# Token groups laid out by batch row and quarter of the steps, one transfer per load, reload and store, in a mixture-of-experts and gated recurrence kernel

## The reference

```
def _L0(x, t_emb, ...):              # on all 8192 tokens
    shared = silu(xf @ w1) * (xf @ w3) @ w2
    s = sigmoid(concat([xf, tf]) @ router_W)
    _, topk_idx = top_k(s + router_bias, 2)      # 2 of 8 experts per token
    gates = s_sel / s_sel.sum()
    h = gelu(einsum('nc,ech->enh', xf, W1e)); y = einsum('enh,ehc->enc', h, W2e)
    return (shared + einsum('ne,enc->nc', combine, y)) / 3
def step(h, z_t):                    # 256 steps in order, all batch rows at once
    gate = sigmoid(h @ Wh.T + z_t @ Wz.T + b)
    h_new = tanh(h * leak + gate * z_t)
    return h_new, h_new
x = x + _L0(x, cond);  x = x + hs    # hs: the states of all steps, z = x
```

## Time and profile before

| | |
|---|---|
| time of three runs | 1169.03, 1170.54, 1175.3 us; median 1170.54 |
| the profiled execution | 1181.83 us, its span 1179.8 us |
| busy in the profiled execution | PE 804.2, DVE 564.8, ACT 452.5, POOL 261.4 us |
| mean granted TensorE clock | 0.837 |
| transfers | 129.65 MB, of them 64 + 64 + 128 issues of x_tok, x_res and out_dram |

### The profile page before, as it was taken

One profiled execution on the slowest core, in us unless ns is written; L12 is line 12 of the kernel. 1 busy time (PEld: TensorE's weight loads), 2 busy tenths in 40 slices (PEclk: granted clock), 3 DMA queues, 4 the chain that ended last, 5 costly groups with the idle time before them and its releaser, 6 DMA issues.

```text
span 1179.8 us, 25116 instructions
## 1 busy us (share of the span) xinstructions
PE 804.2 (68%) x8750; PEld 561.1 (48%) x8750; DVE 564.8 (48%) x2038; ACT 452.5 (38%) x1321; POOL 261.4 (22%) x286
## 2 busy tenths in 40 slices
PE   0655944465974694698379478845958999859653
PEld 0322743443573562367267245734724688425332
DVE  3652413324762352667136357633536754547543
ACT  2341522222542351445145144523524566424333
POOL 1236005615006115100700510052052000340000
PEclk9877976778987797998679798876989999969765
DMA  9683775527344332453542334443334154330001
GB/s 268 183 263 119 190 169 131 157 85 170 68 96 152 95 104 79 105 122 83 147 95 88 93 83 94 92 125 91 86 107 99 39 116 119 112 85 28 10 10 37
DMA packets 203498, 129.65 MB, mean 110 GB/s; under 512 B 138578, under 2 KB 192372, under 8 KB 203380
## 3 DMA queue, kind: packets, MB, share of 16 engines
q1 hardware_dynamic: 188260, 86.03, 30.7%
q0 software_dynamic: 14400, 41.96, 11.1%
q10 hardware_dynamic: 720, 0.05, 0.0%
HBM read 39.90 MB, written 56.62 MB: 82 GB/s over the span
## 4 chain that ended last, share of the span: by engine, by line
PE 41%; another core or an unknown queue 16%; DVE 13%; issue 11%; SPq 8%; ACT 8%; DMA 3%; DVEq 0%; ACTq 0%
PE bank L1525 40%; SPq L797 5%; SPq L779 2%; DVE taken L1359 2%; DVE pre L1362 2%; DVE hid_low L1312 1%; ACT th L1065 1%; ACT hs_high L1073 1%; DMA x_res<-in_x_dram 1%; DVE r_part L1326 1%; PE bank L1693 1%; DVE full L1296 1%; ACT half L1031 1%; DVE left L1214 1%
## 5 line engine op out<-in xcount | busy, mean ns | idle before, releaser
L1525 PE MATMUL bank<-xe,w1e_high 128*128 128x128 f16 x1408 | 235.9, 227 | 45.9 <-issue 26.9
L1359 DVE SCALAR_TENSOR_TENSOR taken<-th,zq 128x64 f32<-128x64 f32 x256 | 57.4, 224 | 301.0 <-ACT th L1065 289.1
L1525 PE MATMUL bank<-xs,w_high 128*128 128x512 f16 x512 | 182.0, 403 | 21.7 <-DVE full L1296 17.5
L1065 ACT ACTIVATE th<-bank 128x64 f32<-128x64 f32 x256 | 56.9, 222 | 330.1 <-PE bank L1525 171.4
L1525 PE MATMUL bank<-hs_high,gwt_high 128*128 128x32 f16 x1024 | 80.6, 180 | 135.2 <-ACT hs_high L1073 106.3
L1525 PE MATMUL bank<-xe,w1e_low 128*128 128x128 f16 x704 | 157.8, 227 | 14.2 <-issue 14.2
L1312 DVE TENSOR_TENSOR hid_low<-full,hid_high 128x512 f16<-128x512 f32 x152 | 104.7, 689 | 120.8 <-ACT hid_high L1018 109.5
L1525 PEld LDWEIGHTS bank<-xe,w1e_high 128*128 x1408 | 123.5, 101 | 75.5 <-issue 59.5
L1525 PEld LDWEIGHTS bank<-hs_high,gwt_high 128*128 128x128 f16 x1024 | 70.5, 99 | 178.7 <-ACT hs_high L1073 129.5
L924 POOL TENSOR_TENSOR fence_pool<-zero 128x1 f32<-128x1 f32 x12 | 2.7, 227 | 673.9 <-issue 246.9
L1073 ACT ACTIVATE hs_high<-pre 128x64 f16<-128x64 f32 x256 | 65.6, 256 | 124.8 <-DVE pre L1362 113.6
(11 more groups left out here) (151 smaller groups left out, 1746.9 us busy)
## 6 DMA issues: line engine op xcount, KB each, us to landing
y_slots_even<-y_pair SPq DMA_DIRECT2D x44, 256.0 KB
y_slots_odd<-y_pair SPq DMA_DIRECT2D x44, 256.0 KB
x_tok<-in_x_dram SPq DMA_DIRECT2D x64, 128.0 KB, 2.9
x_res<-in_x_dram SPq DMA_DIRECT2D x64, 128.0 KB
out_dram<-o_tok SPq DMA_DIRECT2D x128, 64.0 KB
x_slots_even<-zeros POOLq DMA_DIRECT2D x1, 3072.0 KB, 14.8
x_slots_odd<-zeros POOLq DMA_DIRECT2D x1, 3072.0 KB, 11.7
y_got<-in_L_cond_W1e_dram SPq DMA_DIRECT2D x4, 512.0 KB
```

Source lines behind the costliest of these rows:

```text
L1065: nc.scalar.activation(flat3(th[:, s % 2]), gate_sums(s), ACT.Tanh, scale=0.5 / UP).then_inc(s_th, 1)
L1359: dve.scalar_tensor_tensor(flat3(taken[:, s % 2]), flat3(th[:, s % 2]), 1.0, flat3(z_of(s // HALF)[:, s % HALF]), ALU.add, ALU.mult).then_ ...
L1525: return pe.matmul(out_ap, w, mov, start=start, stop=stop, skip_group_check=True)
```

## The change

A tile's partition is now 4 times the batch row plus the quarter t of the group's 16 steps, and tile j of a group holds steps 4t + j. So partition p of a group is four steps in a row of one batch row, 4 KB in DRAM: the load, the reload and the store (2 KB a partition there) are one transfer each, with all 128 partitions. Semaphore counts follow (16 instead of 64 for each group). Where z leaves PSUM and where o_ch is written, the order of tokens is turned back into steps by the access pattern of the same instruction: the innermost loop over the batch rows steps 4 f32 elements in PSUM (`by_token`), and o_ch is written with that step. On SP, `load_res` moves from behind the pair store to the head of the unit. The four tables are written anew; the numbers of operations are the same.

```diff
-    x_in = x.rearrange("b (j t) c -> t b j c", t=TT)
-    out_v = out.rearrange("b (a j t) c -> a t b j c", j=2, t=TT)
+    x_in = x.rearrange("b (q t j) c -> q b t (j c)", t=TT, j=GROUP)
+    out_v = out.rearrange("b (a t j) c -> a b t (j c)", t=TT, j=2)
-        cond_t = sb("cond_t", [P, KC, TT, NB])
+        cond_t = sb("cond_t", [P, KC, NB, TT])
-        o_ch = sb("o_ch", [P, KC, HALF, NB])
+        o_ch = sb("o_ch", [P, KC, 2, NB, TT])
+        def by_step(ap):
+            return ap.rearrange("p (t j) b -> p t j b", j=GROUP)
+        def by_token(bank):
+            return bank[:].rearrange("p (j b t) -> p t j b", b=NB, t=TT)
             def load_x(q):
-                for t in range(TT):
-                    sp.dma_start(x_tok[NB * t:NB * (t + 1), q % NXT, :, :], x_in[t][:, q * GROUP:(q + 1) * GROUP, :]
-                                 ).then_inc(s_x[q % NXT], 16)
+                sp.dma_start(x_tok[:, q % NXT].rearrange("p j c -> p (j c)"), x_in[q]).then_inc(s_x[q % NXT], 16)
             def load_res(q):
-                for t in range(TT):
-                    sp.dma_start(x_res[NB * t:NB * (t + 1), :, :], x_in[t][:, q * GROUP:(q + 1) * GROUP, :]
-                                 ).then_inc(s_res, 16)
+                sp.dma_start(x_res[:].rearrange("p j c -> p (j c)"), x_in[q]).then_inc(s_res, 16)
             def store(c):
-                for t in range(TT):
-                    sp.dma_start(out_v[c, t], o_tok[NB * t:NB * (t + 1), c % 2, :, :]).then_inc(s_out[c % 4], 16)
+                sp.dma_start(out_v[c], o_tok[:, c % 2].rearrange("p j c -> p (j c)")).then_inc(s_out[c % 4], 16)
             def body(u):
+                for q in range(N_GROUPS):
+                    if u.i == FINISH[q] - 2:
+                        load_res(q)
                 if u.kind == EXPERT and u.k + NIN < PAIRS[u.n]:
                     load_pair(u.n, u.k + NIN)
                 prepare(u.i)
                 done = units_at(u.i - DOWN_LAG, EXPERT)
                 if done:
                     store_pair(done)
-                for q in range(N_GROUPS):
-                    if u.i == FINISH[q] - 2:
-                        load_res(q)
...
-                    nc.scalar.activation(zq[:, q % NZQ, :, kc, :], y_ps[kc][:].rearrange("p (t b) -> p t b", b=NB),
+                    nc.scalar.activation(by_step(zq[:, q % NZQ, :, kc, :]), by_token(y_ps[kc]),
                                          ACT.Copy, scale=HALVED).then_inc(s_part if q < EARLY else s_z, 1)
...
-                part = zq[:, q % NZQ, :, kc, :]
-                dve.scalar_tensor_tensor(part, gate_ps[kc][:].rearrange("p (t b) -> p t b", b=NB), HALVED, part,
+                part = by_step(zq[:, q % NZQ, :, kc, :])
+                dve.scalar_tensor_tensor(part, by_token(gate_ps[kc]), HALVED, part,
                                          ALU.mult, ALU.add).then_inc(s_z, 1)
...
-                    ins = dve.scalar_tensor_tensor(o_ch[:, kc], z_of(c)[:, :, kc, :], 2.0,
-                                                   hist[:, some, kc, :], ALU.mult, ALU.add)
+                    ins = dve.scalar_tensor_tensor(o_ch[:, kc].rearrange("p j b t -> p t j b"),
+                                                   z_of(c)[:, :, kc, :].rearrange("p (t j) b -> p t j b", j=2), 2.0,
+                                                   hist[:, some, kc, :].rearrange("p (t j) b -> p t j b", j=2),
+                                                   ALU.mult, ALU.add)
...
-                                                o_ch[:, kc, j * TT:(j + 1) * TT, :].rearrange("p t b -> p (t b)"),
+                                                o_ch[:, kc, j].rearrange("p b t -> p (b t)"),
```

and of the tables, for example in PE_AT:

```diff
-    (34, 8): ((FILL, 0), (STEP, 0),), (35, 4): ((FILL, 1),), (35, 5): ((STEP, 1),), (36, 0): ((STEP, 2),),
+    (34, 7): ((FILL, 0),), (35, 0): ((STEP, 0), (FILL, 1),), (35, 1): ((STEP, 1),), (35, 4): ((STEP, 2),),
```

More of the change, by code:

```diff
@@ new lines @@
+    (43, 11): ((REST, 17),), (44, 2): ((MIX, 18),), (44, 6): ((REST, 18),), (44, 12): ((MIX, 19),),
+    (45, 7): ((REST, 19),), (45, 10): ((MIX, 20),), (45, 12): ((REST, 20),), (46, 6): ((MIX, 21),),
+    (47, 2): ((REST, 21), (MIX, 22), (REST, 22),), (47, 6): ((MIX, 23),), (47, 7): ((REST, 23),),
+    (49, 2): ((MIX, 24), (Z, 7), (REST, 24), (MIX, 25),), (49, 4): ((REST, 25),), (50, 4): ((MIX, 26),),
+    (50, 8): ((REST, 26),), (50, 9): ((MIX, 27),), (51, 2): ((REST, 27),), (51, 7): ((MIX, 28),),
@@ new lines @@
+    (70, 7): ((MIX, 62),), (70, 9): ((REST, 62),), (70, 11): ((MIX, 63),), (71, 1): ((REST, 63),),
+    (71, 10): ((MIX, 64),), (71, 11): ((Z, 12), (REST, 64),), (72, 2): ((MIX, 65),), (72, 8): ((REST, 65),),
+    (72, 13): ((MIX, 66),), (73, 4): ((REST, 66),), (73, 7): ((MIX, 67),), (73, 8): ((REST, 67),),
+    (73, 10): ((MIX, 68),), (73, 12): ((REST, 68),), (74, 3): ((MIX, 69),), (75, 0): ((REST, 69),),
+    (75, 5): ((MIX, 70), (REST, 70),), (76, 0): ((MIX, 71),), (77, 5): ((REST, 71), (MIX, 72),),
@@ new lines @@
+    (77, 8): ((Z, 13), (REST, 72),), (78, 2): ((MIX, 73), (REST, 73), (MIX, 74), (REST, 74),),
+    (78, 4): ((MIX, 75), (REST, 75),), (79, 2): ((MIX, 76),), (79, 4): ((REST, 76),),
+    (79, 7): ((MIX, 77), (REST, 77),), (80, 1): ((MIX, 78), (REST, 78), (MIX, 79),), (80, 9): ((REST, 79),),
+    (81, 1): ((MIX, 80), (REST, 80), (MIX, 81), (REST, 81),), (81, 4): ((MIX, 82),), (81, 6): ((REST, 82),),
+    (82, 1): ((MIX, 83),), (82, 3): ((REST, 83), (MIX, 84), (REST, 84), (MIX, 85), (REST, 85),),
@@ new lines @@
+    (122, 1): ((REST, 163), (Z, 22),), (122, 2): ((Z, 23), (MIX, 164),), (122, 4): ((REST, 164),),
+    (123, 0): ((MIX, 165),), (123, 1): ((REST, 165),), (123, 2): ((MIX, 166),), (123, 6): ((REST, 166),),
+    (123, 8): ((MIX, 167), (REST, 167),), (124, 1): ((MIX, 168),), (124, 3): ((REST, 168),),
+    (124, 9): ((MIX, 169), (REST, 169),), (125, 0): ((MIX, 170),), (125, 2): ((REST, 170),),
+    (125, 5): ((MIX, 171), (REST, 171), (Z, 24), (Z, 25),), (125, 8): ((MIX, 172),), (125, 10): ((REST, 172),),
@@ new lines @@
+    (157, 4): ((REST, 233), (MIX, 234), (REST, 234), (MIX, 235), (REST, 235), (MIX, 236), (REST, 236), (MIX, 237),),
+    (157, 5): ((REST, 237), (MIX, 238), (REST, 238), (MIX, 239),),
+    (157, 7): ((REST, 239), (MIX, 240), (REST, 240), (MIX, 241),), (157, 9): ((REST, 241), (MIX, 242),),
+    (158, 2): ((REST, 242), (MIX, 243),), (158, 6): ((REST, 243),), (158, 7): ((MIX, 244),), (158, 9): ((REST, 244),),
+    (159, 0): ((MIX, 245), (REST, 245), (MIX, 246),),
+    (159, 1): ((REST, 246), (MIX, 247), (REST, 247), (MIX, 248), (REST, 248), (MIX, 249), (REST, 249),),
@@ L390 @@
+    (159, 6): ((MIX, 250),), (159, 7): ((REST, 250),),
+    (159, 8): ((MIX, 251), (REST, 251), (MIX, 252), (REST, 252), (MIX, 253), (REST, 253),), (160, 3): ((MIX, 254),),
+    (160, 4): ((REST, 254),), (160, 5): ((MIX, 255),), (161, 8): ((REST, 255),),
 }
@@ L880, in _ @@
             for part in range(4):
-                sp.wait_ge(s_out[part], 16 * TT * (NSTEP // HALF // 4))
+                sp.wait_ge(s_out[part], 16 * (NSTEP // HALF // 4))
         @block.gpsimd
@@ L1755, in _ @@
             for k in range(KC):
[L1756 removed]
+                last = mm(bank[1][:, 0:E], cond_t[:, k].rearrange("p b t -> p (b t)"), rw[:, KC + k, :],
                           k == 0, k == KC - 1)
```

581 lines of the change are left out of this document (275 added, 306 removed), and 2 rows, old and new, of the table OUT_AT.

## The result

The changed kernel took 1139.97 us in the median of 4 runs (1134.81 to 1145.48), the kernel before 1172.92 us (1169.03 to 1178.95, 4 runs). The ratio is 0.9715, 95% interval [0.9646, 0.9784]: 33 us faster, where 35.5 were forecast for the median.

A forecast was written before the change was run, and what follows sets the result against it. A loop over PE, ACT and DVE, and places where all three stand, set the end. Terms 26.9 + 3.8 + 4.5 + 4.2 + 1.3 - 3 = 37.7 us, less 2, gave 35.5: median 1135 us, profiled 1146.3, 8-in-10 range 1117 to 1157.

The forecast's parts named there:

- The reload at the head: Reload of x_res issued first in SP's unit: all six waits of DVE's r_part for it go, 26.9 us.
- The clock behind the waits: PE's clock, low after each of four long waits, costs 0 to 7.5 us in all; 3.8 us taken as gain.
- One transfer for four: SP's single issues gain 4.5 us at 135 to 162 us, 4.2 at the start, 1.3 at the last store.
- the first transpose ends that much sooner: At the start, weights are issued 2.7 us sooner, so the first transpose behind them ends 2.7 us sooner, near 13.7 us.
- The rival of the issue that is no cheaper: A wide SP issue takes 2 us, not 0.5; only the order gains, 28 us, 1143 us; chance 0.10.
- Strided elements: ACT's zq reads and DVE's o_ch writes at a step of 4: 3 us lost, a tenth of 30.3 us.
- most would lie in idle time: Of 30.3 us added busy time, most is idle time: ACT idle 13.4 us before zq, DVE 3.0 before o_ch.
- Tables and bursts: New tables 0, bounds -5 and +5 us; PE's stops in twelve POOL bursts shift the sum by 8 us either way.
- The differences are taken over as they are: The same 35.5 us comes off the profiled 1181.8 us (to 1146.3) and the median 1170.5 us (to 1135).
- The wait moves: Rival: r_part or the step behind it waits for gathered rows or turned tokens; gain 22 us, 1148 us; chance 0.18.
- The head reload holds up SP: Rival: the reload's wait for DVE delays SP's transposes and pair loads; gain 10 us or less, 1160 to 1170; chance 0.05.
- Strided elements at twice the time or at three times: Rivals for zq and o_ch, all on the path: twice, 10 us gained, 1160, chance 0.09; three times, 1190, slower, chance 0.04.

## Why the prediction was right, step by step

**The reload at the head** (26.9 us, all six waits go). Right: the six waits are gone, and the move alone gains 32.5 us where the kernel before had 36.5 us of such waits, with a lead that grows by the length of the wait at five of the eight. SP's wait for DVE was 2.2 us until 1000 us (1.0 before), so next to nothing was held up behind the head reload. The slack is smaller than the 10 us that I worked out: the reload of the rows above is issued by 461.3 and r_part comes at 474.69, 13.4 us later, and where r_part waited for a reload in one transfer it followed the issue by 3.8 to 8.1 us, which leaves 5.3 to 9.6. "All six waits go" held in the first profile; in the second of the changed kernel one of 1.7 us was left.

**The clock behind the waits** (3.8 us, the middle of 0 and 7.5). Near in size: 1.15, 1.45, 1.65 and -0.3 us behind four of the five waits over 4.5 us (the fifth has the wait for gathered rows behind it), 4.0 in all. The middle of two bounds was a choice and not an argument, so that it came out is in part luck, and that the clock is the cause is argued from its level in the rows.

**One transfer for four** (4.5 + 4.2 + 1.3 = 10.0 us). The three places were right and the parts were not. By the first pair of profiles: start 0.9 us at logits 0, 6.7 by section 1, and 1.6 at the end (from the last th to the end 8.7 us before, 7.2 after): 8.3. The step "the first transpose ends that much sooner" is false: the weights were issued 1.9 us sooner, and the transpose that I let end at 13.7 ended at 17.45. The term rested on the transfers ahead of it being done sooner, and I had no row for what they wait for. At 135 to 162 us the three loads did save 4.5 us of SP's time; 2.0 of it went into longer transposes (17.6 us for three sets in place of 15.7), and PE went on 5.9 us after the first pair's issue for 4.2 before. A wide issue took 0.60 us, where I took 0.5. In the faster kind of session four issues in the new layout cost 12.6 us, for a step of 2.3 us at each and not 1.5; that is the only run in which the number of issues alone changes. The rival of the issue that is no cheaper is refuted, though a narrow one in the new layout is dearer than a wide one.

**Strided elements** (3 us, a tenth of an upper bound of 30.3). This is the term whose reasoning failed. zq costs nothing more; o_ch costs 0.2 us more, 13.1 us and not 16.7; and of that 7.3 us lie on the path, where a tenth would be 1.3. So the term was 7.3 us and not 3; "most would lie in idle time" is false for o_ch. I had judged the cover by the idle time just before o_ch (3.0 us). What stands behind it in DVE's queue was not looked at: in the changed kernel o_ch comes at 36 places (one operation or two), and the next operation is the loop's own hs_low at 16 and taken at 14 of them; at 27 of these 30 it starts within 0.1 us of the end of o_ch, which fits that o_ch held it up.

**Tables and bursts** (0, bounds 5 and 8). The tables are right: 0.9591 and 0.9593 with old and new ones. The bursts are not bounded by 8: PE stood within them for 14.4 us less than before in the first pair of profiles, just under the 15 that the prediction named as a sign against itself, and for 164.4 to 180.3 us in five profiles of changed kernels.

**The sum.** On the terms of the profile 1146.3 was forecast and 1137.2 came, on those of the median 1135 and 1140. "The differences are taken over as they are" is where this splits: the one profiled execution of before was 8.9 us above its median and that of the changed kernel 2.8 below. In the faster kind of session the parts are: move alone 32.5, layout 12.4 with 7.3 of o_ch's stride already paid, both 38.1. They fall short of their sum by 6.8 us; the layout alone had taken 8.7 us off the same waits (36.5 to 27.8), which is enough for it. That the sum of the prediction came within 2.5 us of the 33 measured is in part luck: the issues' term came to 8.3 for 10.0 and the strided one to 7.3 for 3, while the 2 us taken off on top and the chosen middle for the clock made up for a part of it. How the 33 us split in the slower kind is not shown, since the kernels that would split them ran only in the faster one.

**The rivals.** The wait moves: in part, to gathered rows, 4.2 us with the move alone and 5.7 in the changed kernel with the old tables; in the two profiles of the changed kernel itself not at all. The head reload holds up SP: no. Strided elements at twice the time or at three times: o_ch grew by half, zq by nothing.

The page "SBUF — State Buffer" of the Trainium skill, section "Door 1: The DMA port swizzle", which the prediction weighed, asks for at least two hits in a line of 16 bytes of SBUF. The runs agree with that: a step of 2 f32, two hits a line, is free (419 ns), a step of 4, one hit, costs 622. The note gives no size of the penalty; the doubling was the prediction's own upper bound. For PSUM the same note gives 8-byte lines and speaks of matmuls; zq, read from PSUM by ACT and DVE at a step of 4, showed no cost (593 for 595, 684 for 683 ns).

## What to carry to other kernels

When an engine that runs a serial loop waits for a transfer, look up the transfer's place in the queue that issues it before its size: moving one issue ahead of what that queue itself waits for was worth most of its waits (32.5 of 36.5 us), while the layout work was worth 12.4 us alone and 5.6 on top of the move. Price an operation that grows by what stands behind it in its engine's queue too, not by the idle time ahead of it alone. Fewer issues save time only where the chain runs through the issuing queue, and part of it is paid back at the landing.

## What the runs showed of the hardware

**Bursts of POOL and PE.** The earlier trace rows show PE at a near stop (19 matmuls in 23.7 us) while POOL issues its scatters. In the faster kind of session, the same kernel, the same burst and the same stretch of it (it begins at 438.4 us there and at 561.6 in the earlier trace rows):

```profile
449.50:473.20 23.70, 22.83 (x345) 19.65 (x342) 13.17 (x52) 15.44 (x50) 16.34 (x17) 1.00 0.71 210
```

345 matmuls, and POOL as busy as before. Between the two profiles of the kernel before, the lead of the faster is 0.1 us until the first burst, 8 at the start of the second and 251 us at the end; from 330 us on it grows by 178 us over the last seven bursts and what follows right behind them, and between them by less than 5 us in any one stretch. So PE's stop belongs neither to the kernel nor to the burst by itself. What it belongs to is open; the texts recorded ahead of the runs speak of chips, and a device with the same number stood once in each kind. The gain was 33 us in one kind and 38 in the other.

**Issue and landing of a transfer.** The issue is not priced by its bytes: 0.43 us for 32 partitions with rows of 1 KB, 0.67 for 32 with rows of 4 KB, 0.59 for 128 with rows of 4 KB. Issue to landing of x_tok has a median of 2.9 to 3.2 us with four narrow transfers of the old layout and 4.3 to 4.5 with one wide.
